# Attention, cross-attention and FFN on one core: first scores moved ahead of the batch's seam, windows and probabilities moved as rectangles, context steps redistributed

## The reference, cut to what matters

```python
x = x + attn(layernorm(x), ...)              # 8 x 512 x 256, 16 heads of 16, relative positions clipped at 20
x = x + xattn(layernorm(x), ctx, ctx, ...)   # ctx 8 x 1601 x 256, 16 heads of 64, no softmax
x = x + ffn(layernorm(x), ...)               # 704 wide, fp4 quantised in blocks of 16
# attn:   softmax((q k^T + q rel_k[clip(j - i)]^T) / 4) @ v, plus attn @ rel_v[clip(j - i)]; then Wo
# xattn:  qn, kn are q and k of each head over their l2 norm; out = (qn kn^T) v = qn (kn^T v)
#         x = Q + out wo + bo;  x + gelu(ln(x) w1 + b1) w2 + b2
```

## Time and profile before

| | us |
|---|---|
| median of 3 runs | 2904.91 |
| lowest, highest | 2897.34, 2914.84 |
| the profiled execution: its own time | 2905.99 |
| its span, first to last instruction | 2904.1 |
| PE busy in the span | 2529.4 |
| DVE, POOL, ACT busy | 1705.5, 1437.7, 1180.0 |

### The profile page before, as it was taken

One profiled execution on the slowest core, in us unless ns is written; L12 is line 12 of the kernel. 1 busy time (PEld: TensorE's weight loads), 2 busy tenths in 40 slices (PEclk: granted clock), 3 DMA queues, 4 the chain that ended last, 5 costly groups with the idle time before them and its releaser, 6 DMA issues.

```text
span 2904.1 us, 49839 instructions
## 1 busy us (share of the span) xinstructions
PE 2529.4 (87%) x14884; PEld 1734.0 (60%) x14884; DVE 1705.5 (59%) x3890; ACT 1180.0 (41%) x2089; POOL 1437.7 (50%) x1489
## 2 busy tenths in 40 slices
PE   3697899888998889988999889988899888998877
PEld 1365566665665656656566655666566565666645
DVE  4746644676446764566646665367654676456625
ACT  1237423382234722355333642338323472235511
POOL 2447444573545645365553745457344564436422
PEclk8799999998999999999999999999999999999989
DMA  8607200670007600284004720057100760028300
GB/s 244 140 0 167 59 1 8 143 181 25 1 27 166 163 1 1 70 160 126 1 8 100 177 71 1 8 132 181 36 1 22 167 167 1 1 68 160 104 0 8
DMA packets 403729, 224.59 MB, mean 77 GB/s; under 512 B 209822, under 2 KB 399542, under 8 KB 400438
## 3 DMA queue, kind: packets, MB, share of 16 engines
q1 hardware_dynamic: 370406, 215.76, 30.6%
q10 hardware_dynamic: 33024, 5.24, 1.6%
HBM read 129.15 MB, written 91.80 MB: 76 GB/s over the span
## 4 chain that ended last, share of the span: by engine, by line
PE 64%; DVE 9%; DMA 8%; issue 8%; ACT 6%; POOL 3%; SPq 1%; ACTq 0%; DVEq 0%; POOLq 0%
PE PS L1601 58%; PE PS L1604 7%; DMA prob_scr<-arena 5%; DMA arena<-bias_scr 2%; ACT arena L1104 1%; ACT arena L1097 1%; DVE PS L1377 1%; DVE ss L1476 1%; DVE arena L1306 1%; POOL rstd L429 1%; SPq L587 1%; ACT arena L1151 1%; POOL arena L769 1%; DVE arena L1295 1%; DVE css L1285 0%
## 5 line engine op out<-in xcount | busy, mean ns | idle before, releaser
L1601 PE MATMUL PS<-arena 128*17 128x128 f32 (+7 forms) x6656 | 746.5, 310 | 84.4 <-ACT arena L1097 66.9
L1601 PEld LDWEIGHTS PS<-arena 128*17 128x17 f32 (+2 forms) x6656 | 498.7, 123 | 272.8 <-issue 125.8
L1604 PE MATMUL PS<-ident,arena 128*128 128x128 f32 (+1 forms) x3312 | 520.3, 285 | 101.1 <-DVE arena L1299 31.1
L1604 PEld LDWEIGHTS PS<-ident,arena 128*128 128x128 f32 (+1 forms) x3312 | 390.4, 145 | 274.0 <-issue 92.4
L429 POOL TENSOR_TENSOR crn<-crn,mhalf 128x8 f32<-128x8 f32 (+1 forms) x208 | 373.5, 1802 | 115.8 <-DVE crn L1287 114.3
L1377 DVE CUSTOM_DVE_ANT_0 PS<-PS,arena 128x512 f32<-128x512 f32 x512 | 343.0, 711 | 125.1 <-POOL arena L769 89.5
L1601 PE MATMUL PS<-cwk,arena 128*128 128x512 f32 (+1 forms) x832 | 406.9, 613 | 2.6 <-ACT arena L990 2.6
L1097 ACT ACTIVATE arena<-PS,nmax 128x512 f32<-128x512 f32 x512 | 344.8, 695 | 113.7 <-DMA prob_scr<-arena 59.5
L985 ACT ACTIVATE arena<-PS 128x512 f32<-128x512 f32 (+1 forms) x208 | 124.2, 597 | 553.7 <-PE PS L1601 553.7
L769 POOL TENSOR_TENSOR arena<-arena 128x128 f32<-128x128 f32 x512 | 218.0, 459 | 102.7 <-DMA arena<-bias_scr 97.4
L1104 ACT ACTIVATE arena<-PS 128x512 f32<-128x512 f32 x384 | 232.5, 606 | 10.5 <-PE PS L1601 9.4
(11 more groups left out here) (162 smaller groups left out, 3654.9 us busy)
## 6 DMA issues: line engine op xcount, KB each, us to landing
arena<-bias_scr SPq DMA_DIRECT2D x128, 336.0 KB, 3.6
prob_scr<-arena SPq DMA_DIRECT2D x128, 336.0 KB, 4.6
q_scr<-arena SPq DMA_DIRECT2D x128, 128.0 KB
arena<-q_scr SPq DMA_DIRECT2D x128, 128.0 KB, 4.4
arena<-k_scr SPq DMA_DIRECT2D x16, 768.0 KB, 11.9
arena<-prob_scr SPq DMA_DIRECT2D x128, 80.0 KB, 3.4
arena<-far_scr SPq DMA_DIRECT2D x16, 546.0 KB, 7.8
arena<-in_ctx SPq DMA_DIRECT2D x16, 512.0 KB, 5.0
```

Source lines behind the costliest of these rows:

```text
L1601: return pe.matmul(o, l, r, start=start, stop=stop, **kw)
L1604: return pe.transpose(o, i, ident[0:i.shape[0], 0:i.shape[0]])
```

## The change

Eight edits:

1. *Windows and probabilities as rectangles.* The window of rows 0 to 63 is loaded in full (168 wide), that of rows 64 to 127 only from column 64 on (104 wide), in two DMAs. `margins` zeroes the rest, rows 64 to 127, columns 0 to 63, once a batch, with a wait ahead and one behind. `store_probs` writes 104 columns of each half, from column 0 and from column 64, in two DMAs.
2. *Far edges by group.* `far_edge` is one addition of four heads; `far_added` counts groups.
3. *Order on SP.* `load_band` runs two groups behind, across tiles; only the last tile loads its last two bands at once. `store_band` of tiles 2 and 3 is split by group, four parts within tile 0 and four within tile 1.
4. *The seam.* Scores of group 0 stand within `down(3)` between its transposes and its matmuls (`first_scores`). For that `down` uses banks 4 and 5 in place of 0 and 1, and its first tile waits for the fourth `gate_h` in place of the third. SP loads window 0 ahead of all outputs and window 1 behind output 0. POOL makes and adds far edge 0 ahead of pads and values. ACT waits for the pads only at the fourth exps. DVE takes `add_out(2)` before the four first biases and `add_out(3)` behind them.
5. *PE's loop* runs from the norm to the norm: `rest(b)` (from the transposes of the normed rows on), then `attention(b + 1)`.
6. *DVE's loop* holds the two late `add_out` within `batch`.
7. *ACT's copy of the attended rows* runs a tile ahead of the context step (`copy_attended`).
8. *Context steps.* "ln" keeps step 2 of 2 to 5; ("x", -1) has 3 to 6 in place of 6 to 8, ("x", 0) 7 to 9 for 9 to 11, ("x", 1) 10 to 12 for 12 to 14, ("x", 2) 13 to 15 for 15 and 16, ("x", 3) 16 to 18 for 17 and 18.

Cut to the changed lines; the bodies moved from `batch` into `scores` on PE are shown once.

```diff
@@ -66,6 +66,8 @@
+HP = 64
+HWIN = HP + BAND
@@ -77,8 +79,8 @@
-   ("wo", 0): (-2,), ("wo", 1): (-1,), ("wo", 2): (0,), ("wo", 3): (1,), "ln": (2, 3, 4, 5),
-   ("x", -1): (6, 7, 8), ("x", 0): (9, 10, 11), ("x", 1): (12, 13, 14), ("x", 2): (15, 16), ("x", 3): (17, 18),
+   ("wo", 0): (-2,), ("wo", 1): (-1,), ("wo", 2): (0,), ("wo", 3): (1,), "ln": (2,),
+   ("x", -1): (3, 4, 5, 6), ("x", 0): (7, 8, 9), ("x", 1): (10, 11, 12), ("x", 2): (13, 14, 15), ("x", 3): (16, 17, 18),
@@ -504,11 +506,15 @@
-  def store_band(eng, nb, t):
+  def store_band(eng, nb, t, lo=0, hi=H):
-      eng.dma_start(bias_scr[t].rearrange("h (p r) -> p h r", r=SKEW)[:, :, 0:BAND],
-                    Rb[:, t, :, 0:BAND]).then_inc(bias_stored[t], 16)
+      eng.dma_start(bias_scr[t, lo:hi].rearrange("h (p r) -> p h r", r=SKEW)[:, :, 0:BAND],
+                    Rb[:, t, lo:hi, 0:BAND]).then_inc(bias_stored[t], 16)
+  def bands_stored(nb, t, g):
+      return 16 * (nb + 1) + 1 if t < 2 else 16 * (NG * nb + g + 1) + 1
@@ -582,11 +588,12 @@
-    sp.wait_ge(bias_stored[t], 16 * (nb + 1) + 1)
+    sp.wait_ge(bias_stored[t], bands_stored(nb, t, g))
-    sp.dma_start(Wn[:, (g % 2) * HG:(g % 2 + 1) * HG, 0:WIN],
-                 bias_scr[t, g * HG:(g + 1) * HG, 0:128 * WIN]
-                 .rearrange("h (p r) -> p h r", r=WIN)).then_inc(win_loaded[g % 2], 16)
+    rows_of = bias_scr[t, g * HG:(g + 1) * HG, 0:128 * WIN].rearrange("h (p r) -> p h r", r=WIN)
+    for lo, c in ((0, 0), (HP, HP)):
+        sp.dma_start(Wn[lo:lo + HP, (g % 2) * HG:(g % 2 + 1) * HG, c:WIN], rows_of[lo:lo + HP, :, c:WIN])\
+            .then_inc(win_loaded[g % 2], 16)
@@ -657,11 +664,14 @@
-     sp.dma_start(prob_scr[t, g * HG:(g + 1) * HG, 0:128 * WIN].rearrange("h (p r) -> p h r", r=WIN),
-                  P[:, (g % 2) * HG:(g % 2 + 1) * HG, t * 128:t * 128 + WIN]).then_inc(p_stored[g % 2], 16)
+     rows_of = prob_scr[t, g * HG:(g + 1) * HG, 0:128 * WIN].rearrange("h (p r) -> p h r", r=WIN)
+     for lo in (0, HP):
+         sp.dma_start(rows_of[lo:lo + HP, :, lo:lo + HWIN],
+                      P[lo:lo + HP, (g % 2) * HG:(g % 2 + 1) * HG, t * 128 + lo:t * 128 + lo + HWIN])\
+             .then_inc(p_stored[g % 2], 16)
-     sp.wait_ge(p_stored[g % 2], 16 * ((b * T + t) * 2 + g // 2 + 1) + 1)
+     sp.wait_ge(p_stored[g % 2], 32 * ((b * T + t) * 2 + g // 2 + 1) + 1)
@@ -677,11 +687,15 @@
-         if g:
-             load_band(t, g - 1)
-         if g == 1 and t < 2:
-             store_band(sp, b, t + 2)
-     load_band(t, NG - 1)
+         if g > 1:
+             load_band(t, g - 2)
+         elif t:
+             load_band(t - 1, g + NG - 2)
+         if t < 2:
+             store_band(sp, b, t + 2, g * HG, (g + 1) * HG)
+     if last:
+         load_band(t, NG - 2)
+         load_band(t, NG - 1)
...
@@ -702,13 +716,13 @@
+    if not final:
+        first_window(b + 1, 0, quant_v)
-        first_window(b + 1, 0, quant_v)
+        first_window(b + 1, 1, quant_c)
-    if not final:
-        first_window(b + 1, 1, quant_c)
...
@@ -752,7 +766,7 @@
-    pool.wait_ge(far_added, m * HG + 1)
+    pool.wait_ge(far_added, m + 1)
@@ -762,11 +776,10 @@
-    pool.wait_ge(win_loaded[g % 2], 16 * ((nb * T + t) * 2 + g // 2 + 1) + 1)
+    pool.wait_ge(win_loaded[g % 2], 32 * ((nb * T + t) * 2 + g // 2 + 1) + 1)
-    for j in range(HG):
-        edge = Wn[:, (g % 2) * HG + j, BAND:WIN]
-        pool.tensor_tensor(edge, edge, Eb[:, j, :], ALU.add).then_inc(far_added, 1)
+    edges = Wn[:, (g % 2) * HG:(g % 2 + 1) * HG, BAND:WIN]
+    pool.tensor_tensor(edges, edges, Eb, ALU.add).then_inc(far_added, 1)
@@ -798,10 +811,15 @@
-   def margins(g):
+   def margins(nb, g):
+       pool.wait_ge(margins_zero, 5 * nb + (2 if g == 0 else 4) + 1)
+       pool.sem_inc(waits_alone, 1)
+       pool.memset(Wn[HP:128, g * HG:(g + 1) * HG, 0:HP], 0.0).then_inc(margins_zero, 1)
+       pool.wait_ge(margins_zero, 5 * nb + (3 if g == 0 else 5) + 1)
+       pool.sem_inc(waits_alone, 1)
...
@@ -949,19 +967,20 @@
-     margins(0)
+     margins(b + 1, 0)
-     margins(1)
+     margins(b + 1, 1)
+     make_far(b + 1, 0, 0)
+     far_edge(b + 1, 0, 0)
-     for g in range(2):
-         make_far(b + 1, 0, g)
-         far_edge(b + 1, 0, g)
+     make_far(b + 1, 0, 1)
+     far_edge(b + 1, 0, 1)
@@ -1090,8 +1109,8 @@
-         act.wait_ge(p_stored[g % 2], 16 * (tile * 2 + g // 2) + 1)
-     if t == 0 and h == 0:
+         act.wait_ge(p_stored[g % 2], 32 * (tile * 2 + g // 2) + 1)
+     if t == 0 and h == HG - 1:
@@ -1135,12 +1154,17 @@
-    for t in range(T):
+    def copy_attended(t):
+    copy_attended(0)
+    for t in range(T):
+        if t + 1 < T:
+            copy_attended(t + 1)
@@ -1358,9 +1382,9 @@
-       dve.tensor_tensor(yout[:, t, :], x2[:, t, :], bank(t % 2, 0, E), ALU.add).then_inc(out_ready, 1)
-   def batch(b, final):
+       dve.tensor_tensor(yout[:, t, :], x2[:, t, :], bank(4 + t % 2, 0, E), ALU.add).then_inc(out_ready, 1)
+   def batch(b, final, prev=None):
@@ -1370,7 +1394,8 @@
-     dve.wait_ge(far_added, u + 2)
+     if j == 0:
+         dve.wait_ge(far_added, tile * NG + g + 2)
@@ -1400,10 +1425,14 @@
-    dve.wait_ge(margins_zero, 3 * (b + 1) + 1)
+    dve.wait_ge(margins_zero, 5 * (b + 1) + 1)
+    if prev is not None:
+        add_out(prev, 2)
+    if prev is not None:
+        add_out(prev, 3)
...
@@ -1743,28 +1768,29 @@
+   def scores(b, t, h):
+       g, j = divmod(h, HG)
+       u = (b * T + t) * H + h
+       near = min(t * 128 + FAR, S)
+       if j == 0:
+           pe.wait_ge(q_loaded[g], 16 * (b * T + t + 1) + 1)
+       if t or g:
+           pe.wait_ge(probs_ready, u - HG + 2)
+       i = mm(bank(j, 0, near), Qp[:, h, :], Kp[:, h, 0:near], True, True)
+       if near < S:
+           i = mm(bank(j, near, S), Qp[:, h, :], Kfar[:, h, near - FAR:NFAR], True, True)
+       i.then_inc(scores_ready, 1)
+   def first_scores(nb):
+       pe.wait_ge(r_act, 2 * T * (nb + 1) + 1)
+       pe.wait_ge(k_loaded, 16 * 2 * len(LOADS_K) * (nb + 1) + 1)
+       for h in range(HG):
+           scores(nb, 0, h)
+   def attention(b, final):
@@ -1802,9 +1828,9 @@
-        scores(t, h + HG)
+        scores(b, t, h + HG)
-        scores(t + 1, h + HG - H)
+        scores(b, t + 1, h + HG - H)
@@ -1814,9 +1840,9 @@
+    pe.wait_ge(out_ready, T * b + 1)
+    pe.sem_inc(waits_alone, 1)
-    for h in range(HG):
-        scores(0, h)
@@ -1879,6 +1905,11 @@
+   def rest(b, final):
+       def slots(at):
+           for s in () if final else SLOTS_AT[at]:
+               slot(b + 1, s)
@@ -1972,14 +2003,16 @@
+     if t == T - 1 and not final:
+         first_scores(b + 1)
-         pe.wait_ge(hh_ready, T * b + 4)
+         pe.wait_ge(hh_ready, T * (b + 1) + 1)
-         i = mm(bank(t % 2, 0, E), hqT[0:w, t % 2, c, :], wdT[0:w, c, :], c == 0, c == NFF - 1)
+         i = mm(bank(4 + t % 2, 0, E), hqT[0:w, t % 2, c, :], wdT[0:w, c, :], c == 0, c == NFF - 1)
@@ -2014,9 +2047,14 @@
-   with pe.Fori(0, NB - 1) as b:
-       batch(b, False)
-   batch(NB - 1, True)
+   first_scores(0)
+   attention(0, False)
+   with pe.Fori(0, NB - 2) as b:
+       rest(b, False)
+       attention(b + 1, False)
+   rest(NB - 2, False)
+   attention(NB - 1, True)
+   rest(NB - 1, True)
```

More of the change, by code:

```diff
@@ L848, in _ @@
             pool.wait_ge(m_act, 4 + 1)
-            margins(0)
-            margins(1)
+            margins(0, 0)
+            margins(0, 1)
             pads(0)
@@ L1587, in _ @@
             with dve.Fori(0, NB - 2) as b:
-                add_out(b, 2)
-                add_out(b, 3)
-                batch(b + 1, False)
-            add_out(NB - 2, 2)
-            add_out(NB - 2, 3)
-            batch(NB - 1, True)
+                batch(b + 1, False, b)
+            batch(NB - 1, True, NB - 2)
             add_out(NB - 1, 2)
```

22 lines of the change are left out of this document (2 added, 20 removed).

## The result

| | before | after |
|---|---|---|
| median of 11 runs | 2903.02 us | 2891.94 us |
| lowest, highest | 2897.34, 2915.46 | 2882.79, 2899.81 |
| span of the profiled execution | 2904.1 | 2887.0 |

The ratio after to before is 0.995 (95% interval 0.9933 to 0.9966): 0.5% faster, some 14 us of 2903 (the medians lie 11 apart), where the forecast was 2846 us, 2% faster, with its own range from 2825 to 2870. A second series on another chip gave 0.9953 (0.9933 to 0.9973).

The account below looks back on a forecast made before the run. It took attention to be held by edge additions waiting for windows through SyncE's order, and TensorE to bound the rest. Attention -68, seam -14, copies -11, moved steps +34 gave -59: 2846 us from 2905, range 2825 to 2870.

Parts of the forecast that it names:

- order on SyncE: Attention: of 12.2 us a batch of edge-addition waits for windows, 10.2 won, 3.2 held back for late windows.
- pace 4.12 to 4.02: Attention: a group falls from GpSimd's 4.12 us to TensorE's 4.02, 1.5 us a batch.
- copies: Output projection: copying attended rows a tile ahead removes two of three TensorE waits, 11 us in all (0 to 19).
- seam and loops: Seam of two batches: first exps come sooner, 2.0 us taken at each of seven, 14 us (4 to 22).
- moved steps: Norm and context steps: uncovered norm and a TensorE wait for `scale_q(0)` cost 34 us (0 to 50).
- the windows' chain: Attention: issue, landing, sum and bias take 7.9 us per two groups, 3.95 a group, leaving TensorE's 4.02 as limit.
- (4): Attention: windows late in every group, the pair landing 1.4 us later, 4.65 a group; 2927 us, chance 0.11.
- (2): Attention: half the window waits stay, SyncE and queue almost full, windows lagging in tiles 0 and 1; 2882 us, chance 0.14.
- (3): Attention: SyncE's store wait becomes a wait of the exps, attention gains nothing; 2914 us at most, chance 0.11.
- (1): Norm and context steps: the moved steps cost nothing, only the 3.44 us stall goes; 2812 us, chance 0.18.
- The signs named beforehand: Whole kernel: GpSimd's window wait under 40 us, SyncE's store wait under 20; wrong if attention's pace exceeds 4.2 a group.
- queue time: DMA queue in attention: rectangles save 6.7 ns on each of 768 rows a group, 0.32 us.

Follow-up runs that it names:

- heads: The changed kernel with edit 2 alone undone (far edges added head by head, rectangles kept): 0.9903 of the kernel before.
- slots0: The changed kernel with edit 8 undone (context steps at their places of before): 0.9842 of the kernel before.
- single_slots0: The changed kernel with edits 1 and 8 undone (single DMAs, context steps at their old places): 0.972 of the kernel before.
- b_order: The kernel before with edit 3 alone (SyncE's order; single DMAs, edges head by head): 0.9795 of the kernel before.
- single: The changed kernel with edit 1 undone (windows and probabilities in one DMA each again): 0.9797 of the kernel before.
- single_heads: The changed kernel with edits 1 and 2 undone (single DMAs, far edges head by head): 0.9741 of the kernel before.
- b_order_copy: The kernel before with edits 3 and 7 (SyncE's order, attended rows copied a tile ahead): 0.9718 of the kernel before.
- best: The changed kernel with edits 1, 2 and 8 undone, leaving SyncE's order, seam, loops and copies: 0.9651 of the kernel before.
- early: The changed kernel with edits 1 and 8 undone and store_band of tiles 2 and 3 issued by ScalarE before attention: 0.9811 of the kernel before.

## Why the prediction was wrong, point by point

Sums in us of 2903, from the ratios above. The kernels of the last column form one chain from before to after, so the measured column adds up to the whole by construction; the kernels beside the chain (`heads`, `slots0`, `single_slots0`) are what tests it.

| term | prediction | measured | from |
|---|---|---|---|
| order on SyncE (edit 3) | -56 (82 won, 26 left) | -60 | b_order |
| pace 4.12 to 4.02, with edits 1, 2 | -12 | +60: rectangles +44 to +47, group-wise sum +14 to +16 | single, heads, single_heads |
| copies (edit 7) | -11 | -22 (by the waits -11) | b_order_copy |
| seam and loops (4 to 6) | -14 | -19 | best against b_order_copy |
| moved steps (edit 8) | +34 | +22 to +31 | slots0, single_slots0, best |
| sum | -59 | about -14 | |

**The step that failed** is the windows' chain in attention: issue 0.25 us after the bias, landing 3.1, sum 1.28, bias of four heads 3.2, together 7.9 or 3.95 a group, under TensorE's 4.02, which was to be the limit. Sum and biases were right (1.28 and 3.21). The other parts were not:

- *Landing.* 3.1 was taken from the windows of one quiet stretch of tile 2. The pair was given the same, since its second half has half the packets. It measured 3.78 in tile 3 and 4.53 in tile 1. Fewer bytes save little and the second issue comes 0.64 later; in tiles 0 and 1 the rows of `store_band` add another 0.9 (`early` against `single`).
- *Issue.* 0.25 holds where SyncE is free. With 7 issues SyncE's turn is 4.8 us, not 3.8: 0.54 was the distance of two single issues of different kinds, while a pair measured 1.26. In tile 1 the window is then issued 0.90 after the bias, on average.
- *Between the parts.* From the landing to the start of the sum pass 0.18 us, from its end to the first bias 0.26. The chain of the prediction has neither: 0.44 us a ring, 0.22 a group.

With them, two groups take 9.0 in tiles 2 and 3 and 10.06 in 0 and 1, 4.52 and 5.03 a group. Even `early`, whose windows in tile 3 are issued after 0.23 and land in 3.16, runs its ring in 8.35, 4.18 a group. The limit was the chain, not TensorE, so the 0.85 us by which the group-wise sum delays the first bias had a price as well, as `heads` and `single_heads` show. The prediction had both in its sums but under the limit of 4.02, where they cost nothing.

**The rivals.** (4), windows late in every group by a longer landing of the pair, named the mechanism: it had 4.65 a group, measured 4.78 on average of 5.03 and 4.52. Worked out again with that, 0.76 over 4.02 in 128 groups is 97 us, 26 of them already held back for tiles 0 and 1: 2846 + 71 = 2917, less 16 by which copies and seam gave more, less some 7 by which the moved steps cost less: 2894, where 2892 was measured. That it comes so near is partly luck: it has attention lose 3 us where the starts of `edge_mass` have it win 6, and it takes the larger figure for the copies. (2) comes near with 2882 and has half of the mechanism: SyncE full in tiles 0 and 1, but windows came late in tiles 2 and 3 too. (3) fell: the exps wait less for the store, 16.0 for 59.5; its time with half the cost of the steps is 2897 and not 2905. (1) fell, the moved steps cost. The signs named beforehand pointed right: SyncE's wait, the first exps at the seam, copies and `scale_q` came as said; GpSimd's wait, to fall under 40 us, rose to 126.5, and the pace over 4.2, named as what would make it wrong, is what came.

**The order** was right in mechanism and size, the residue of 0.4 us a group in tiles 0 and 1 too: `b_order` runs 4.56 there and 4.13 in the others.

**The moved steps** were right: from the last of the norm's rows (1043.70) to the end of the first projection (1053.91) after takes 10.2 us, 9.6 forecast; the wait for `scale_q(0)` 2.15 of 2.5. The low clock behind that second hole mostly stayed away, it came in one batch of seven; behind the first it came in all seven, 5.2 to 6.5 us for 3.70, where 1.7 more were counted.

**The copies** came as said by the traces and at twice that by the ratio. The prediction held back 1.1 of the 2.7 us because VectorE was close behind. The ratio gave 22, known to about 8 and taken between two chips. The waits fell by 17.6 and rose by 6.5 behind them: 11 net, so VectorE did hold back what was said. What else the 22 would hold is not shown.

**The seam** gave about what was said, 19 for 14, known to about 10; which part of edits 4 to 6 gives it was not tried.

**Slips in its sums.** From 22.5 ns at 160 B and 25.8 at 415 B the slope puts 672 B at 29 ns, not 33, so the rectangles would save half of the 0.32 us of queue time. The 4.88 us of the earlier trace rows span two issues of `load_band`, so the wait is some 0.7 less. Neither carries the forecast.

Not settled: why windows whose rows are all wide land 0.34 us later in tile 3, where the saved queue time is 256 x 7 ns / 16 = 0.1 us by the prediction's slope, and half of that by the corrected one. The packets' durations in the queue may not be additive, but no run here takes that apart.

## What to carry to other kernels

Where a buffer is refilled through DRAM behind a compute step, write down the whole ring (release, issue, landing, use) with the landing taken at the load that the queue will have, and compare it with the busiest engine before pricing anything as covered. Cutting a transfer in two to save bytes pays only if bytes set its landing: here a third of the bytes landed 0.6 us sooner, and the second issue cost 0.64. And test edits that touch one ring singly: one edit of eight was worth 60 us and two others in the same ring gave it back. A wait that goes away is a gain only if none grows behind it: look at the next wait of the same engine too.
